# A decoder layer on one Trainium2 core: the stage behind the attention begun in its last units, and expert products with features along the partitions

## The chip, the core and the metric

The kernel runs on one core of a Trainium2 chip. Its engines are TensorE (PE, with its weight loads shown apart as PEld), VectorE (DVE), ScalarE (ACT), GpSimd (POOL) and SyncE (SP), which here only issues DMAs. The metric is the device time of one execution in microseconds. The kernel has a program of its own for each engine; the programs meet only at semaphores.

## What is computed

One decoder layer on x of 4 x 1024 tokens, 512 features, all in fp32, with three residual sums:

```
x = x + attention(layernorm(x))            # 16 heads of 64, rotary, causal; W_out 1024 -> 512
x = x + memory_read(layernorm(x), context) # a 32x32 matrix per head built from 64 context rows
                                           # by a recurrence; q normalised, read, Wo, bo
x = x + experts(layernorm(x))              # 8 experts, top 2 of them per token:
        ff_gate = ragged_dot(sorted_tokens, we_gate, group_sizes)
        ff_up = ragged_dot(sorted_tokens, we_up, group_sizes)
        activated = silu(ff_gate) * ff_up
        ff_out = ragged_dot(activated, we_down, group_sizes) * sorted_weights
        output = zeros.at[sorted_token_idx].add(ff_out)
```

Gate, up and down are 512 x 512 for each expert.

## The kernel before

Four stages stand in one launch: context, attention, memory, experts. Each ends with a meeting of all engines (L103 to L110). Tiles called early_... live across stages: early_xT, early_wq and early_wv (weights in split form), early_stage (raw weights), early_ident.

**Products.** An fp32 product is three fp32r products. ACT rounds an operand to a high half (Copy), DVE or POOL subtracts to get the low half, and PE adds high x high, high x low and low x high (three lines: L1601 to L1603 in the memory stage, L2068 to L2070 in the experts).

**Attention (a_...)** goes through U = 512 units: 64 head groups (hg) of 8 query tiles. A unit is scores (PE L950, L951), row maximum (DVE L1216), exponentials (ACT L1084), transposes (PE L962), copies (ACT L1095, DVE L1226) and values (PE L979, ACT L1101, DVE L1241). The queries and keys of a head group come from a_rot over 12 DMAs of 128 KB, which SP issues (`stack`, L677 and L681) up to a group ahead, into one of two buffers; scores of the group's first unit wait for all of them. POOL rotates queries and keys (L799, L806), runs the recurrence of the context rows (`context_row`, L850 to L864, ten instructions each, two rows in every 16 units, at units 11 and 14 of them), and at unit U-16 issues `load_next` (L840): the raw weights of the memory stage, six DMAs of 512 KB into early_stage. After the last unit POOL stores the memory matrix (L886). SP stores attention outputs to scr_attT and, per batch, the reciprocals of the row sums to scr_rinv (L696); ACT and DVE turn nothing of the next stage's data in this stage.

**Memory (m_...)** goes through 32 token tiles. For tile i: attention output and reciprocals come in (SP L1471, L1474, 1 MB together), POOL multiplies them (`att_scale`, L1550), ACT and DVE split the product into m_ap (L1706, L1798), PE multiplies by W_out (`att_out`, 24 matmuls of 128x512 in m_A), DVE adds x (L1844) and normalises (L1803 to L1812), PE transposes (`turn`, L1612), multiplies by Wq (m_Q), reads the memory, and so on to router and scatter. At the stage's head POOL writes constants (L1522 to L1544), ACT and DVE split four chunks of W_out in early_xT (L1700, L1776) and centre and split two chunks of Wq in early_wq and early_wv (L1784 to L1788, L1765, L1776). `att_out` of tile 0 waits for the split W_out and for m_ap.

**Experts (e_...)** go through NBLK = 39 blocks of 256 rows (two row tiles t). In a block, PE's order is gate(t0), up(t0), gate(t1), `turn_act`(t0), up(t1), `turn_rows`(t0), half of down(t0), `turn_act`(t1), rest of down(t0), `turn_rows`(t1), down(t1). Gate, up and down are 12 matmuls of 128x512 per row tile, 72 in a block; hT (rows, transposed) stands still and the weight moves. `turn_act` transposes the activation e_a (4 transposes) into PSUM, from where ACT and DVE split it into e_aT (L2136, L2187). `turn_rows` (L2076) transposes the next block's rows. ACT applies silu (L2146), splits the next weights (L2142) and scales the result (L2151); DVE multiplies (`mult`, L2199), splits weights (L2193), and makes the row numbers dest (L2233), which waits for the semaphore `added`, raised when the last block's rows have been added to the output. POOL fetches weights (L2030) and adds rows to the output (`add_rows`, L2034, from e_y and e_dest).

Of the kernel before, what the change touches and what calls it, by code (L numbers as in the profile page):

```python
# [47 lines left out]
def program(nc, io):  # L48
# [19 lines left out]
    with ExitStack() as keep:  # L68
# [5 lines left out]
            "ident": keep.enter_context(nc.sbuf_tensor("early_ident", [P, P], F32)),  # L74
        }
# [355 lines left out]
def attention_phase(nc, io, dram, scan, early):  # L431

    with Room(nc, "a_") as rm:
# [10 lines left out]
        rot = rm.sb("rot", [P, 4, T], F32R)  # L444
# [61 lines left out]
        s_wm = rm.sem("wm")  # L506
        s_scan = rm.sem("scan")
# [72 lines left out]
        def sums_turn(u):  # L580

            if u >= GU * G and u % (GU * G) == 4:
                return u // (GU * G) - 1
            return None


# [80 lines left out]
        def _(sp):  # L667
# [58 lines left out]
            for half in range(2):  # L726
                for b in range(B):
# [3 lines left out]
                                 ).then_inc(s_k2, 16)  # L731
            for u in range(U + 6):
                if values_turn(u - 1) is not None:
                    store(values_turn(u - 1))
                if u % (2 * QT) in (0, QT + 2) and 0 < u < U - QT:
                    stack(u // QT + 1)
                if sums_turn(u - 1) is not None:
                    store_sums(sums_turn(u - 1))
# [12 lines left out]
        def _(gp):  # L751
# [114 lines left out]
            for u in range(U):  # L866
# [12 lines left out]
                if u == U - 16:  # L879
                    load_next()  # L880
                if u == 9:
                    context_start()
                if u % (2 * QT) in (11, 14):
                    context_row(2 * (u // (2 * QT)) + u % (2 * QT) // 14)
            for a in range(2):
                gp.dma_start(dram["mem"][:, :, a * half:(a + 1) * half, :].rearrange("b h i j -> (b h) (i j)"),  # L886
                             M[a * 64:(a + 1) * 64, :, :].rearrange("p i j -> p (i j)")).then_inc(s_mem, 16)
            gp.wait_ge(s_mem, 32)
            gp.wait_ge(s_wm, 96)

# [153 lines left out]
        def _(act):  # L1044
# [61 lines left out]

            key_root(0)
# [6 lines left out]
            for u in range(U + 6):  # L1114
# [10 lines left out]
                for n, j in ends(v_steps(u - 1), 8):  # L1125
                    v_high(n, j)

        @block.vector
        def _(dve):
# [112 lines left out]

            key_variance()
# [10 lines left out]
            for u in range(U + 6):  # L1254
# [22 lines left out]
                if u < U:  # L1277
                    for p in splits(u):
                        if p[0] == "x":
                            x_low(p)  # L1280

# [7 lines left out]
def memory_phase(nc, io, dram, route, early):  # L1289
# [4 lines left out]
    with Room(nc, "m_") as rm:  # L1294
# [5 lines left out]
        ap = rm.sb("ap", [P, 2, 2, 8, P], F32R)  # L1300
# [32 lines left out]
        sd = rm.sb("sd", [P, 2])  # L1333
        rs = rm.sb("rs", [P, 2])
# [44 lines left out]
        def weights(a, k):  # L1379

            return early["xT"][:, a, k, :] if k < ET else (
                early["wq" if k == ET else "wv"][:, a, :, :].rearrange("p e n -> p (e n)"))
# [76 lines left out]
        def _(sp):  # L1459
# [35 lines left out]
            load_att(0, 0)  # L1495
            load_x(0, 0)
            for dst, src in ((bo[:, :], io["bo"].partition_broadcast(P)),
                             (wo[:, :, :], io["woT"].rearrange("(e p) n -> p e n", p=P))):
                sp.dma_start(dst, src).then_inc(s["c"], 16)
            load_att(0, 1)  # L1500
            load_x(0, 1)
# [794 lines left out]
```

## Time and profile before

| | us |
|---|---|
| median of three runs | 2873.59 |
| the runs | 2867.46, 2873.59, 2874.5 |
| the profiled execution | 2874.91 |
| its span | 2873.2 |
| PE busy, share of the span | 2665.0, 93% |
| DVE busy | 2000.5, 70% |
| ACT busy | 1620.8, 56% |
| POOL busy | 1468.0, 51% |

The span is the time between the first and the last recorded instruction; 1.7 us of the profiled execution lie around it. Time in rows is counted from the span's start. Attention ends and memory starts at about 1595; experts start at about 2131. A row of a timeline gives the start, the length, the engine, the line, the operation with its tiles, how many instructions of a kind follow in it, and in brackets how long the engine had been idle and for whom it waited. Matmuls are pipelined, so the next one starts before the end shown: what a matmul costs is the distance of two starts.

### The profile page before, as it was taken

Reading aid. Unit: us, or ns where it says so; the run is one execution under the profiler, and the core shown is the slowest. Engines: PE = TensorE matmul, PEld = TensorE weight load, DVE = VectorE, ACT = ScalarE, POOL = GpSimd, SP = SyncE. Lnnn points to the kernel's source line nnn. Section 1 sums busy time; section 2 is a strip of 40 time slices with the busy share of each in tenths; the row PEclk is TensorE's granted clock in tenths of the full one; section 3 lists DMA queues with packets and bytes.
Section 4 is the critical chain, followed back from the end, with each engine's and each line's share of the span. In section 5 each row is a group of like instructions: output and inputs, shape, how many; then the busy total and the mean of one; then the engine's idle time right before and its main releaser. Section 6 shows DMA issues by size and latency. Waiting matters only on the chain. (4 is left out here: it accounts for less than half of the span.)

```text
span 2873.2 us, 48962 instructions
## 1 busy us (share of the span) xinstructions
PE 2665.0 (93%) x15375; PEld 2267.7 (79%) x15375; DVE 2000.5 (70%) x4223; ACT 1620.8 (56%) x3157; POOL 1468.0 (51%) x1676
## 2 busy tenths in 40 slices
PE   7999989999899999899998599999959999999997
PEld 5888878888788888788887487877748888888886
DVE  6777766777667777677777688978846556666655
ACT  3666666666656666566666333333336666666665
POOL 3676646676647675556565333434323444343434
PEclk9999999999999999999999799999979999999999
DMA  6654544444544444444444654544334443444433
GB/s 175 106 122 106 123 103 98 118 113 104 132 96 99 115 107 114 103 109 100 94 91 114 170 135 134 158 134 147 96 126 96 102 87 74 102 99 100 100 52 51
DMA packets 192360, 316.56 MB, mean 110 GB/s; under 512 B 60496, under 2 KB 106224, under 8 KB 189104
## 3 DMA queue, kind: packets, MB, share of 16 engines
q1 hardware_dynamic: 148656, 216.86, 31.6%
q0 software_dynamic: 43520, 97.46, 13.9%
q8 instruction: 90, 1.47, 0.2%
q14 instruction: 94, 0.77, 0.1%
HBM read 241.08 MB, written 75.17 MB: 110 GB/s over the span
## 5 line engine op out<-in xcount | busy, mean ns | idle before, releaser
L1095 ACT ACTIVATE a_pt<-a_PT 128x512 fp32r<-128x512 f32 (+3 forms) x768 | 350.4, 491 | 449.9 <-PE a_PT L962 443.3
L1226 DVE TENSOR_TENSOR a_pt<-a_PT,a_pt 128x512 fp32r<-128x512 f32 (+3 forms) x768 | 401.5, 550 | 155.2 <-ACT a_pt L1095 150.7
L1216 DVE CUSTOM_DVE_ANT_0 a_S<-a_S,a_mask 128x1024 f32<-128x1024 f32 (+7 forms) x512 | 387.5, 757 | 72.5 <-PE a_S L951 71.1
L1084 ACT ACTIVATE a_pb<-a_S,a_nmax 128x1024 f32<-128x1024 f32 (+7 forms) x512 | 381.0, 744 | 36.5 <-DVE a_nmax L1216 36.5
L962 PE MATMUL a_PT<-early_ident,a_pb 128*128 128x128 f32 x2304 | 345.0, 276 | 51.2 <-DVE a_pt L1226 50.9
L962 PEld LDWEIGHTS a_PT<-early_ident,a_pb 128*128 128x128 f32 x2304 | 275.9, 142 | 112.4 <-issue 58.5
L979 PE MATMUL a_O<-a_pt,a_v 128*128 128x256 f32 (+1 forms) x2560 | 346.5, 283 | 17.8 <-DVE a_xt L1201 16.8
L979 PEld LDWEIGHTS a_O<-a_pt,a_v 128*128 128x128 f32 x2560 | 330.4, 193 | 31.2 <-DVE a_xt L1201 24.0
L2193 DVE TENSOR_TENSOR e_w<-early_stage,e_w 128x1024 fp32r<-128x1024 f32 x238 | 280.6, 1220 | 65.0 <-ACT e_w L2142 64.9
L950 PE MATMUL a_S<-a_kh,a_qs 128*128 128x512 f32 (+3 forms) x768 | 286.7, 373 | 10.6 <-DMA a_kl<-a_rot 8.8
L951 PE MATMUL a_S<-a_kl,a_qs 128*128 128x512 f32 (+3 forms) x768 | 259.0, 349 | 0.0
L2034 POOL DMA_INDIRECT out<-e_y,e_dest x78 | 158.3, 2029 | 183.5 <-ACT e_y L2151 157.5
L894 PE MATMUL a_Z<-early_xT,early_wq 128*128 128x512 f32 x512 | 226.1, 442 | 26.5 <-DVE early_stage L1189 18.4
L2142 ACT ACTIVATE e_w<-early_stage 128x2048 fp32r<-128x2048 f32 x120 | 229.2, 1911 | 31.5 <-DVEq L2177 19.3
L806 POOL TENSOR_TENSOR a_rot<-early_stage,a_rot 128x512 fp32r<-128x512 f32 x128 | 163.4, 1295 | 146.3 <-ACT a_rot L1066 146.1
L1241 DVE TENSOR_TENSOR a_ot<-a_O,a_otmp 64x256 f32<-64x256 f32 x256 | 106.2, 415 | 184.1 <-ACT a_otmp L1101 184.0
L2030 POOL DMA_INDIRECT early_stage<-in_we,e_ix x119 | 128.1, 1076 | 177.7 <-issue 163.5
L799 POOL TENSOR_TENSOR early_stage<-early_stage,a_part 128x512 f32<-128x512 f32 x64 | 82.6, 1291 | 265.8 <-DVE a_part L1189 265.7
L895 PE MATMUL a_Z<-early_xT,early_wq 128*128 128x512 f32 x512 | 203.2, 397 | 0.0
L896 PE MATMUL a_Z<-early_xT,early_wq 128*128 128x512 f32 x512 | 203.2, 397 | 0.0
L950 PEld LDWEIGHTS a_S<-a_kh,a_qs 128*128 128x128 f32 x768 | 147.4, 192 | 32.9 <-DMA a_kl<-a_rot 12.3
L951 PEld LDWEIGHTS a_S<-a_kl,a_qs 128*128 128x128 f32 x768 | 147.5, 192 | 17.1
(305 smaller groups left out, 6890.2 us busy)
## 6 DMA issues: line engine op xcount, KB each, us to landing
a_qs<-a_rot SPq DMA_DIRECT2D x256, 128.0 KB, 2.4
a_kh<-a_rot SPq DMA_DIRECT2D x256, 128.0 KB, 2.4
a_kl<-a_rot SPq DMA_DIRECT2D x256, 128.0 KB, 2.4
e_rows<-scr_hs SPq DMA_DIRECT2D x40, 516.0 KB
scr_attT<-a_ot SPq DMA_DIRECT2D x256, 64.0 KB, 2.2
m_att<-scr_attT SPq DMA_DIRECT2D x32, 512.0 KB
m_rb<-scr_rinv SPq DMA_DIRECT2D x64, 256.0 KB
early_stage<-in_wqk POOLq DMA_DIRECT2D x31, 512.0 KB
```

The costliest lines, as they stand in the source:

```text
L894: pe.matmul(out, lhs(0), rhs(0), start=start, stop=False)
L895: pe.matmul(out, lhs(0), rhs(1), start=False, stop=False)
L950: pe.matmul(out, q, kh[:, sl, c0:c1], start=True, stop=False)
L951: mm = pe.matmul(out, q, kl[:, sl, c0:c1], start=False, stop=True)
L962: mm = pe.transpose(PT[(k + s) % 2][:, (kt % 4) * P:(kt % 4 + 1) * P], pb[u % 2][:, kt * P:(kt + 1) * P], ident[:, :])
L979: mm = pe.matmul(O[:, c0:2 * P], v2[:, n % 2, kt, h, :, :].rearrange("p a d -> p (a d)"), pt[j % 2][:, part, kt, c0:2 * P], start=kt == 0 ...
L1084: act.activation(pb[u % 2][:, 0:cols], S[u % 2][:, 0:cols], ACT.Exp, bias=nmax[:, u % GU:u % GU + 1], scale=-1.0, accum_out=rsum[:, b % 2, ...
L1095: act.activation(pt[u % 2][:, 0, 4 * s:4 * s + m, (qt % 2) * P:(qt % 2 + 1) * P], PT[(k + s) % 2][:, 0:m * P].rearrange("p (k q) -> p k q" ...
L1216: dve.tensor_tensor_reduce(out=sc, in0=sc, in1=mask[:, T - cols:T], scale=-1.0, scalar=-MASKED, op0=ALU.add, op1=ALU.min, accum_out=nmax[: ...
L1226: dve.tensor_tensor(pt[u % 2][:, 1, 4 * s:4 * s + m, q], PT[(k + s) % 2][:, 0:m * P].rearrange("p (k q) -> p k q", k=m), pt[u % 2][:, 0, 4 ...
L2142: act.activation(w[:, k, 0, :], raw[:, k, :], ACT.Copy).then_inc(s[f"whi{k}"], 1)
L2193: dve.tensor_tensor(w[:, k, 1, c], raw[:, k, c], w[:, k, 0, c].bitcast(F32), ALU.subtract).then_inc(s[f"wlo{k}"], 1)
```

## The change

Three groups of edits; line numbers in orders "after" are those of the changed kernel.

**1. The attention's last units.** a_rot becomes early_rot and is kept; in the memory stage it is `ap`. SP loads attention outputs and reciprocals of tiles 0 and 1 at units U-13 and U-11, POOL multiplies them at U-8 and U-6, ACT and DVE split them into early_rot behind the last units. Four chunks of W_out are split at U-7 to U+1, the high half by ACT, the low half by POOL. Four context rows move into earlier 16-unit stretches (24 to 27), so that the last one stands at U-34 and the store of the matrix at U-32. The reciprocals of the last batch are turned and stored two units earlier.

```diff
+        ROWS_AT = [u for u in range(U) if u % (2 * QT) in (11, 14) or
+                   u % (2 * QT) == 2 and 24 <= u // (2 * QT) < 28][:TC]
+        FRONT_IN = (U - 13, U - 11)
+        FRONT_SCALE = (U - 8, U - 6)
+        TAIL_HIGH = (U - 7, U - 5, U - 3, U - 1)
+        TAIL_LOW = (U - 5, U - 3, U - 1, U + 1)
...
+            def tail_low(k):
+                gp.wait_ge(s_wmhi, k + 1)
+                gp.tensor_tensor(xT[:, 1, k, :], tail(k), xT[:, 0, k, :].bitcast(F32),
+                                 ALU.subtract).then_inc(s_wmlo, 1)
...
+            def tail_high(k):
+                act.wait_ge(s_wm, 96)
+                act.activation(xT[:, 0, k, :], tail(k), ACT.Copy).then_inc(s_wmhi, 1)
+
+            def front_high(j):
+                act.wait_ge(s_fscale, j + 1)
+                for sl in range(2):
+                    act.wait_ge(s_stack[sl], 192 * (NG * GH // 2))
+                act.activation(front[:, j, 0, :, :], front_rows(j), ACT.Copy).then_inc(s_fhi, 1)
```

On POOL, near the attention's end, the rows L864 and L852 to L862 are context rows, early_stage<-in_wmem is `load_next`, L806 (now L860) the low half of the last rotation. Before:

```order
1106 L864 TENSOR_TENSOR scan_keys<-scan_keys 128x512
1107 L840 DMA early_stage<-in_wmem 128x1024 x6
1108 L852 TENSOR_TENSOR scan_keys<-scan_keys,scan_k 128x512
...
1127 L864 TENSOR_TENSOR scan_keys<-scan_keys 128x512
1128 L886 DMA scr_mem<-scan_keys 64x512 x2
```

After:

```order
1120 L918 TENSOR_TENSOR scan_keys<-scan_keys 128x512
1121 L956 DMA scr_mem<-scan_keys 64x512 x2
...
1126 L854 TENSOR_TENSOR early_stage<-early_stage,a_part 128x512
1127 L860 TENSOR_TENSOR early_rot<-early_stage,early_rot 128x512 x2
1128 L894 DMA early_stage<-in_wmem 128x1024 x6
1129 L923 TENSOR_TENSOR a_xt<-a_xt,early_wq 128x1024
1130 L923 TENSOR_TENSOR a_part<-a_part,early_wq 128x1024
1131 L928 TENSOR_TENSOR early_xT<-early_stage,early_xT 128x1024 x4
```

No context row stands between the last rotation and `load_next` any more; two multiplications and four subtractions stand behind it.

**2. The head of the memory stage.** PE no longer waits there for the split W_out nor for POOL's constants; tiles 0 and 1 are neither loaded, multiplied nor split; only the two chunks of Wq are centred and split. The raw weights of the first expert are fetched at tile 2. ACT applies one root first, which loads its table. On PE, behind `att_out` of tile 0 (24 matmuls), the transposes of tile 0's normalised rows stood ahead of `att_out` of tile 1. Before:

```order
6243 L1603 MATMUL m_A<-early_xT,m_ap 128x512
6244 L1612 MATMUL m_T<-early_ident,m_n 128x128 x4
6245 L1601 MATMUL m_A<-early_xT,m_ap 128x512
```

After:

```order
6243 L1693 MATMUL m_A<-early_xT,early_rot 128x512
6244 L1691 MATMUL m_A<-early_xT,early_rot 128x512
...
6255 L1693 MATMUL m_A<-early_xT,early_rot 128x512
6256 L1702 MATMUL m_T<-early_ident,m_n 128x128 x4
6257 L1691 MATMUL m_A<-early_xT,early_rot 128x512
```

They stand behind 12 of the second tile's 24 matmuls now.

**3. The experts.** Gate and up are computed with their features along the partitions: a 128x128 piece of the weight stands still, the 256 transposed rows move. `turn_act` goes; the activation is split from SBUF, in halves h of the features. Down is cut into four pieces of six matmuls.

```diff
-                for e in range(ET):
-                    mm = parts(out[t][:, :], lambda a: hT[:, t, a, e * P:(e + 1) * P],
-                               lambda a: w[:, k, a, e * D:(e + 1) * D], e)
+                for f in range(2 * h, 2 * h + 2):
+                    for e in range(ET):
+                        c = e * D + f * P
+                        mm = parts(out[h][:, f % 2 * BLK:(f % 2 + 1) * BLK], lambda a: w[:, k, a, c:c + P],
+                                   lambda a: hT[:, a, e, :], e)
...
                 product(j, 0, pG, 0, "G")
+                product(j, 0, pG, 1, "G")
                 product(j, 1, pU, 0, "U")
-                product(j, 0, pG, 1, "G")
-                turn_act(j, 0)
                 product(j, 1, pU, 1, "U")
+                down(j, 0, 0)
                 turn_rows(j + 1, 0)
-                down(j, 0, 0, 2)
-                turn_act(j, 1)
-                down(j, 0, 2, ET).then_inc(s["Y"], 1)
+                down(j, 1, 0)
                 turn_rows(j + 1, 1)
-                down(j, 1, 0, ET).then_inc(s["Y"], 1)
+                down(j, 0, 1)
+                down(j, 1, 1)
...
+            def act_high(j, h):
+                act.wait_ge(s["mul"], 2 * j + h + 1 + CR)
+                act.wait_ge(s["Y"], 2 * j + CR)
+                act.activation(aT[:, 0, 2 * h:2 * h + 2, :], a32[:, h, :].rearrange("p (f r) -> p f r", f=2),
+                               ACT.Copy).then_inc(s["ahi"], 1)
...
+            def act_low(j, h):
+                dve.wait_ge(s["ahi"], 2 * j + h + 1)
+                f = slice(2 * h, 2 * h + 2)
+                dve.tensor_tensor(aT[:, 1, f, :], a32[:, h, :].rearrange("p (f r) -> p f r", f=2),
+                                  aT[:, 0, f, :].bitcast(F32), ALU.subtract).then_inc(s["alo"], 1)
```

On PE, the end of the up product in the last block (before: up(t1) comes after `turn_act`(t0), L2083). Before:

```order
7157 L2070 MATMUL e_G<-e_w,e_hT 128x512
7158 L2083 MATMUL e_T<-early_ident,e_a 128x128 x4
7159 L2068 MATMUL e_U<-e_w,e_hT 128x512
```

After:

```order
7215 L2158 MATMUL e_U<-e_hT,e_w 128x256
7216 L2159 MATMUL e_U<-e_hT,e_w 128x256
7217 L2184 REGISTER_ALU
7218 L2157 MATMUL e_Y<-e_w,e_aT 128x512
```

The matmuls of gate and up are half as wide and twice as many, 96 in a block, and down follows them with no transposes of e_a between. On DVE, one block's loop, first the multiplication. Before:

```order
3042 L2199 TENSOR_TENSOR e_a<-e_U,e_sil 128x512
3043 L2187 TENSOR_TENSOR e_aT<-e_T,e_aT 128x512
...
3046 L2199 TENSOR_TENSOR e_a<-e_U,e_sil 128x512
3047 L2233 CAST e_dest<-e_nxt 128x2
```

After:

```order
3042 L2287 TENSOR_TENSOR e_a<-e_U,e_sil 128x512
3043 L2275 TENSOR_TENSOR e_aT<-e_a,e_aT 128x512
3044 L2320 CAST e_dest<-e_nxt 128x2
...
3051 L2281 TENSOR_TENSOR e_w<-early_stage,e_w 128x1024
3052 L2285 REGISTER_ALU
3053 L2287 TENSOR_TENSOR e_a<-e_U,e_sil 128x512
3054 L2275 TENSOR_TENSOR e_aT<-e_a,e_aT 128x512
```

dest, with its wait for `added`, and half a weight split stand ahead of the second multiplication now. On POOL the fetch of the gate weight stands ahead of the first `add_rows`.

## Rows read from the trace of the kernel before

**Rows 1.** The page: busy us, share of the span, instructions by engine.
```profile
PE 2665.0 (93%) x15375; PEld 2267.7 (79%) x15375; DVE 2000.5 (70%) x4223; ACT 1620.8 (56%) x3157; POOL 1468.0 (51%) x1676
```

**Rows 2.** Timeline of PE, one expert block: start us, length us, engine, line, operation.
```profile
2400.12 0.39 PE L2068 MATMUL e_G<-e_w,e_hT 128*128 128x512 f32 x1
...
2402.91 0.60 PE L2083 MATMUL e_T<-early_ident,e_a 128*128 128x128 f32 x4
2403.27 0.48 PE L2068 MATMUL e_U<-e_w,e_hT 128*128 128x512 f32 x1
2403.58 0.40 PE L2069 MATMUL e_U<-e_w,e_hT 128*128 128x512 f32 x1
...
2418.64 0.39 PE L2068 MATMUL e_G<-e_w,e_hT 128*128 128x512 f32 x1
```

**Rows 3.** Timeline of PE, 256-column matmuls with a new stationary operand each.
```profile
59.97 0.28 PE L896 MATMUL a_Z<-early_wv,early_xT 128*128 128x256 f32 x1
...
62.49 0.28 PE L896 MATMUL a_Z<-early_wv,early_xT 128*128 128x256 f32 x1
```

**Rows 4.** Timeline of DVE in the same expert block.
```profile
2406.44 0.69 DVE L2199 TENSOR_TENSOR e_a<-e_U,e_sil 128x512 f32<-128x512 f32 x1 [1.52 <-PE e_U L2070]
2407.05 0.16 DVE L2233 CAST e_dest<-e_nxt 128x2 int32<-128x2 f32 x1
...
2407.67 1.22 DVE L2193 TENSOR_TENSOR e_w<-early_stage,e_w 128x1024 fp32r<-128x1024 f32 x1
```

**Rows 5.** The line L2034, add_rows: from issue to landing, us.
```profile
DMA to landing us min/median/max: 4.6/4.9/9.5
```

**Rows 6.** Timeline of the memory stage's head, POOL, PE and DVE.
```profile
1595.23 0.52 POOL L1522 MEMSET m_bd<- 128x512 f32 x1 [29.97 <-POOLq L110]
...
1607.58 0.76 PE L1601 MATMUL m_A<-early_xT,m_ap 128*128 128x512 f32 x1 [16.91 <-DVE m_ap L1798]
...
1615.06 0.40 PE L1603 MATMUL m_A<-early_xT,m_ap 128*128 128x512 f32 x1
1623.55 1.11 PE L1612 MATMUL m_T<-early_ident,m_n 128*128 128x128 f32 x4 [8.09 <-DVE m_n L1812]
...
1632.37 0.69 DVE L1844 TENSOR_TENSOR m_x<-m_A,m_x 128x512 f32<-128x512 f32 x1 [4.87 <-PE m_A L1603]
...
1634.68 2.35 DVE L1812 TENSOR_SCALAR m_n<-m_x,m_mv,m_rs 128x512 f32<-128x512 f32 x1
```

**Rows 7.** Windows: length; PE, PEld, DVE, ACT, POOL busy; PEclk; DMA share; GB/s.
```profile
1607.00:1611.00 4.00, 3.42 (x8) 2.77 (x9) 3.90 (x5) 0.88 (x1) 0.00 (x0) 0.50 1.13 192
```

**Rows 8.** Timeline near the attention's end, POOL, SP (DMA issues) and PE.
```profile
1533.20 1.26 POOL L852 TENSOR_TENSOR scan_keys<-scan_keys,scan_k 128x512 f32<-128x512 f32 x1
...
1547.04 3.20 POOL L840 DMA_DIRECT2D early_stage<-in_wmem  x6 [0.30 <-POOL scan_keys L864]
...
1533.27 0.57 SPq L677 DMA_DIRECT2D a_qs<-a_rot  x1
...
1539.59 1.22 SPq L681 DMA_DIRECT2D a_kl<-a_rot  x2
...
1542.65 0.50 PE L950 MATMUL a_S<-a_kh,a_qs 128*128 128x512 f32 x1
```

**Rows 9.** From issue to landing: a_kl issued 1549 to 1554, then the six wmem DMAs.
```profile
DMA to landing us min/median/max: 7.9/8.6/9.7
...
DMA to landing us min/median/max: 5.0/10.6/15.5
```

**Rows 10.** Timeline of PE and DVE, first units of the last two head groups.
```profile
1562.91 0.50 PE L950 MATMUL a_S<-a_kh,a_qs 128*128 128x512 f32 x1 [2.82 <-DMA a_kl<-a_rot]
...
1543.88 1.23 DVE L1216 CUSTOM_DVE_ANT_0 a_S<-a_S,a_mask 128x1024 f32<-128x1024 f32 x1
...
1549.02 1.10 DVE L1216 CUSTOM_DVE_ANT_0 a_S<-a_S,a_mask 128x896 f32<-128x896 f32 x1
...
1564.15 1.23 DVE L1216 CUSTOM_DVE_ANT_0 a_S<-a_S,a_mask 128x1024 f32<-128x1024 f32 x1 [2.88 <-PE a_S L951]
...
1571.36 1.10 DVE L1216 CUSTOM_DVE_ANT_0 a_S<-a_S,a_mask 128x896 f32<-128x896 f32 x1 [0.71 <-PE a_S L951]
```

**Rows 11.** Timeline of ACT: a split of 128x1024, then an attention copy.
```profile
1605.17 1.06 ACT L1706 ACTIVATE m_ap<-m_att 128x1024 fp32r<-128x1024 f32 x1 [5.83 <-issue]
...
1579.23 0.38 ACT L1101 ACTIVATE a_otmp<-a_O 64x256 f32<-64x256 f32 x1 [0.72 <-PE a_O L979]
```

More of the change, by code:

```diff
@@ L74, in program @@
             "ident": keep.enter_context(nc.sbuf_tensor("early_ident", [P, P], F32)),
+            "rot": keep.enter_context(nc.sbuf_tensor("early_rot", [P, 4, T], F32R)),
         }
@@ L506, in attention_phase @@
         s_wm = rm.sem("wm")
+        s_wmhi = rm.sem("wmhi")
+        s_wmlo = rm.sem("wmlo")
+        s_first = [rm.sem(f"first{i}") for i in range(2)]
+        s_fscale = rm.sem("fscale")
+        s_fhi = rm.sem("fhi")
+        s_flo = rm.sem("flo")
         s_scan = rm.sem("scan")
@@ L580, in sums_turn, with front_rows, front_sums, tail @@
         def sums_turn(u):
-            if u >= GU * G and u % (GU * G) == 4:
+            if u == U + 2:
+                return B - 1
+            if GU * G <= u < U and u % (GU * G) == 4:
                 return u // (GU * G) - 1
             return None
+        front = rot[:, :, :].rearrange("p (j a) (f t) -> p j a f t", j=2, t=P)
+        def front_rows(j):
+            return (xt[:, :, :, :].rearrange("p a e t -> p (a e) t") if j == 0 else
+                    part[:, :, :].rearrange("p a (f t) -> p (a f) t", t=P))
+        def front_sums(j):
+            return wq[:, j, :, :].rearrange("p e n -> p (e n)").bitcast(F32)
+        def tail(k):
+            return stage[:, k // 2, k % 2 * T:(k % 2 + 1) * T]
+        ROWS_AT = [u for u in range(U) if u % (2 * QT) in (11, 14) or
[4 more added lines that the diff above has]
+        TAIL_LOW = (U - 5, U - 3, U - 1, U + 1)
         def values_done(u):
@@ L1562, in step @@
                     gp.tensor_tensor(x2b[:, i % 4, :], x2[:, i % 2, :], bo[:, :], ALU.add).then_inc(s["x2b"], 1)
-                if here(r, i + 2):
+                if here(r, i + 2) and after(r, i + 2, 3):
                     att_scale(r, i + 2)
+                if isinstance(r, int) and t == 2:
+                    gp.wait_ge(s["wl"], 2)
+                    for k in range(3):
+                        gp.dma_start(route["raw"][:, k, :], io["we"][0, k]).then_inc(s["pre"], 16)
                 if here(r, i - 4):
@@ L1633, in memory @@
                               ).then_inc(s["mwp"], 1)
-                if here(r, i - 1):
+                second = isinstance(r, int) and r * QT + i == 1
+                if here(r, i - 1) and not second:
                     turn("n", 1, n2[:, (i - 1) % 2, :], "n2")
@@ L1697, in _ @@
             act.sem_inc(s["hT"], CR)
-            act.sem_inc(s["ahi"], CR)
-            for k in range(4):
-                act.activation(weights(0, k), loaded(k), ACT.Copy).then_inc(s["wh"], 1)
-            act.wait_ge(s["pool"], 18)
+            act.sem_inc(s["ahi"], CR + 2)
+            act.activation(root[:, :], ident[:, 0:1], ACT.Sqrt)
             def att_high(r, j):
                 t = r * QT + j
-                act.wait_ge(s["an"], t + 1)
+                act.wait_ge(s["an"], t - 1)
                 act.wait_ge(s["x2"], t - 1 + CR)
@@ L1736, in step @@
                 memory_high(1)
-                if here(r, i + 1):
+                if here(r, i + 1) and after(r, i + 1, 2):
                     att_high(r, i + 1)
@@ L1836, in step @@
                 memory_low(1)
-                if here(r, i + 1):
+                if here(r, i + 1) and after(r, i + 1, 2):
                     att_low(r, i + 1)
@@ L2048, in _ @@
                 point(j + 2)
-                wait_alone(gp, s["y"], 2 * j + 1 + CR, s["any"])
-                add_rows(0)
                 wait_alone(gp, s["ix"], j + 2, s["any"])
@@ L2053, in _ @@
                 fetch(0)
+                wait_alone(gp, s["y"], 2 * j + 1 + CR, s["any"])
+                add_rows(0)
                 wait_alone(gp, s["y"], 2 * j + 2 + CR, s["any"])
```

193 lines of the change are left out of this document (108 added, 85 removed).

## The prediction, made before the changed kernel ran

> **What bounds the kernel now.** I read the page first: PE is busy for 2665.0 of 2873.2 us, 93%, and the next engine, DVE, for 70% [rows 1]. So time is to be had in two ways only: from waits of PE, or from the work that PE does. Then the timeline of PE in the three places that the change touches. In the experts the matmuls follow each other without a gap [rows 2]: that stage is bound by PE's own work, and only fewer or cheaper matmuls shorten it. At the head of the memory stage PE stands still for 16.91 and then 8.09 us [rows 6]: there the chain POOL, ACT, DVE is the bound. Near the attention's end PE waits once, 2.82 us, for the keys of the last head group [rows 10], and the transfers are what counts there. The rest of the program is not changed in anything that PE waits for.
>
> **The experts.** A block lasts from 2400.12 to 2418.64, 18.52 us [rows 2]. From the first gate matmul to the transposes there are 12 matmuls in 2.79 us, 0.233 each. From the start of the four transposes to the second matmul behind them it is 0.67, of which 0.233 is the first matmul's: a group of transposes costs 0.44. With 72 matmuls and four groups, 72 x 0.233 + 4 x 0.44 = 18.54, the block as measured.
> The change makes 48 of the 72 into 96 of 256 columns, each with a weight piece of its own to load. The context of such matmuls is in the trace: 21 of them in a row from 59.97 to 62.49, 0.120 apart [rows 3], their loads hidden. So 96 x 0.120 = 11.52 in place of 48 x 0.233 = 11.18: the turned products cost 0.34 more. The two groups of `turn_act` go, 0.88. The new block is 11.52 + 24 x 0.233 + 2 x 0.44 = 17.99, 0.54 less; 39 blocks give **-21.0**. If each narrow matmul took just half a wide one, 0.1165, it would be another 0.34 less per block, 13 in all; if 0.123, 0.29 more, 11 in all. I take 0.120, which is the same form and the same shape.
> This holds if the split of the activation is in time, because the transposes and halves that covered it are gone. From the block's start: G ends at 5.76, U's first half at 8.64, its second at 11.52. `mult` starts 0.3 behind the half's end and lasts 0.69 [rows 4], to 9.6; the high half on ACT takes about 0.6 (1.06 for twice the size [rows 11]), the low half on DVE 0.7, done at about 11.0. down starts at 11.52: 0.5 spare. DVE then makes dest (0.62 from there to the weight split, 1.22 for that) [rows 4], to 12.7; the second `mult` ends at 13.4, high 14.1, low 14.8. The down pieces that need it start behind two pieces of six (1.40 each) and two groups of transposes: 11.52 + 2.80 + 0.88 = 15.2. Spare, 0.35. This is the thinnest cover of the change: what DVE does later than so is lost in each block. The last rows of the next block are split at about 17.2, wanted at 18.0.
> The `added` signal moves ahead of the second `mult` on DVE; behind it in DVE's queue wait the weight split, `mult`, and through them ACT's splits and down. I place the issue of the second `add_rows` at 4.5 us into the next block (two row results on ACT behind the block's end, then two adds on POOL), an estimate, and its landing 4.9 later (4.6 to 9.5) [rows 5], 9.4. DVE reaches the wait at about 10.9. 1.5 spare, 1.8 until PE waits.
>
> **The head of the memory stage.** Nothing that `att_out` of tile 0 needs is made in the stage any more, so PE starts within 0.3 us of the stage's first record at 1595.23, not at 1607.58 [rows 6]. It starts at half clock as before: 8 matmuls in the window 1607 to 1611 stood 0.43 apart with PEclk 0.50 [rows 7], which is 1.2 of 2.4 GHz, after PE had been idle. The 24 matmuls then take 7.7 as before (1607.58 to 1615.3) and end at 1603.3. Half of tile 1 follows at once, 12 x 0.233 = 2.8, to 1606.1. Meanwhile DVE adds x and normalises: for tile 1 it was 2.3 from the addition at 1632.37 to the last step at 1634.68, and 2.35 for that step [rows 6]. From 1603.9 on this gives 1606.6 (a last step of 0.4) to 1608.6. Transposes 0.4, 12 more matmuls 2.8: tile 1 is out at about 1610.5, where before it was at 1632.37 [rows 6]. I take 21.9 less 0.6 for the normalising step: **-21.3**. The bounds: 17, if DVE's steps are all held up beside POOL and PE falls back to half clock for a piece (12 x 0.2 = 2.4 and 2); 24, if the clock rises earlier. Waits that stand later in the stage are as before, and both chains begin from tile 1.
> The rule against it: 2.35 us for a normalising step of 128x512 on DVE [rows 6], while POOL multiplied, where the addition of 128x512 took 0.69. By the Trainium skill, page SBUF — State Buffer, section Who interferes with whom, DVE and GpSimd share a pair of SBUF ports, and the one that comes second fully blocks until the first has finished. The rows agree. By it the changed stage, where POOL multiplies tile 2 at about 1604 to 1607, loses the same 2 us again.
>
> **The attention's end.** Here the change moves work into a stretch in which PE has little idle time.
> (a) `load_next` moves. Before, it stood behind two context rows on POOL and issued at 1547.04; these rows started at 1533.20, when the last rotation was done [rows 8]. Now nothing stands between, and the six DMAs (3 MB) issue at 1533.3, together with SP's 12 DMAs of head group 62 (1533.27 to 1540.8), whose keys PE wanted at 1542.65 and had [rows 8]. What the two do to each other is seen one head group later: the last four of group 63's key DMAs, issued beside wmem, landed 7.9 to 9.7 us after their issue, the first at 1557.4, the last at 1562.9, with a query DMA among them: five steps of 1.1 us; wmem's took 5.0 to 15.5 [rows 9], from 1552.0 to 1565.2, 2.6 us for each 512 KB. At 1.1 us group 62's 12 are complete at 1546.5, at 1.25 (the first ones wait for the queue to fill) at 1548.3, which I take. PE waits 5.6 us at 1542.65. Behind the wait of before PE ran at half clock and two units took 7.21 us (1564.15 to 1571.36) where they had taken 5.14 (1543.88 to 1549.02) [rows 10]: 2.1 more. Together +7.7.
> (b) In return the old wait goes: wmem has landed at about 1551, well ahead of group 63: -2.8 - 2.1 = -4.9 [rows 10].
> (c) Four high halves on ACT, 1.06 each [rows 11], stand ahead of attention copies that PE waits for. Idle time of ACT hides the first; ACT had 0.7 idle ahead of the copy at 1579.23 [rows 11] and less at its neighbours, so I count 0.7, 0.3 and 1.0 for the others: +2.0. Nothing at the lower end, 4 x 1.06 = 4.2 at the upper.
> (d) Everything else lies beside waits: POOL's six steps (2.4 each, idle there), the front loads (2 MB, when no keys are in flight), the splits into early_rot behind the last units. The stage's end hangs on the stores of the last outputs, as before: 0.
> Sum **+4.8**, from -4.9 (no wait at all, ACT hidden) to +9.
>
> **The rivals.**
> (A) Group 62 is hardly late. SP's keys issue one by one, and if the two streams share the engines equally, keys have their full share: 512 KB in 2.6 us and 128 KB in 1.1 [rows 9] are 200 and 119 GB/s, half of the sum is 160, and the group's 1.57 MB at that take 9.9 us, so they are there at 1543.2 to 1545. Wait 1 to 2.5 us plus clock: +3 or so in place of 7.7, time 2874.9 - 1.3 + 0.1 - 42.3 = 2831. Against it: group 63 saw 1.1 us per DMA, which is 12 x 1.1 = 13.2. Chance 0.22. The Trainium skill, DMA: Bandwidth & Descriptors, section Queues, rings and completion order, states that each engine goes round robin between queue rows packet by packet, which speaks for such an equal share; the time by it would be this rival's.
> (B) The split of the activation is late for the second half of down. Decides from 0.35 us over my chain, for instance by a slower `mult` or by ACT still in its weight split (1.9 us) when `mult` ends. At 0.5 us lost in each block, +20: 2856. Chance 0.12.
> (C) Slower than before: `added` comes late in every block. It decides from 1.8 us later than placed, at 11.2 in the block. Each further us costs 39. From 2.8 us late (over 12.2) the experts lose what all has gained; were every add as long as the longest, 9.5 [rows 5], it would be the landing 4.6 later and 2.8 x 39 = 109 more, 2945. For it: the longest landing is that long, and POOL's queue has a new order. Against: the median is 4.9. Chance 0.03.
> (D) The head gives only 17: 2840, inside the range. Chance 0.13.
> (E) The 256-column matmuls don't keep their rate over 96 in a row, 0.123 or more: +11, 2847. Chance 0.10.
>
> **How the numbers follow.** 2874.9 + 4.8 - 21.3 - 21.0 = 2837.4 for the profiled execution, which lies 1.3 above the median of the runs: **2836**, chance of the sum as it stands 0.40, the rivals have the rest. The range 2823 to 2852 holds the sum with all bounds of the attention's end and the head (2836 - 13 for A with a quicker head and narrow matmuls at half a wide one's; 2836 + 16 for D or E with an attention's end of +9), and leaves out B in its full size, and C: 0.8. About 0.3% or 8.6 us is what a measurement can tell from no change. Faster (below 2865) 0.92; within 0.3% 0.05, from B with more than 0.7 us per block; slower 0.03, C.
>
> **What would show it.** After: expert blocks 18.0 us apart, gate and up matmuls 0.12 apart, no wait of PE for DVE's e_aT at the third piece of down, and none of DVE at dest. Memory: PE's first matmul within 1 us of the barrier, tile 1 added at about T + 15, T being the stage's start. Attention: PE idle for a_kl at the first unit of group 62, not of 63; group 62's DMAs landing over 7 us after their issue. Wrong it would be if PE waits in each block, or if the stage's start T itself moves by more than 6.

## The result, and the profile after

| | before | after |
|---|---|---|
| median, us | 2874.05 (4 runs) | 2835.12 (4 runs) |
| lowest to highest | 2867.46 to 2880.41 | 2831.72 to 2842.36 |
| profiled execution | 2874.91 | 2831.72 |
| its span | 2873.2 | 2830.0 |

The ratio is 0.9874, 95% interval 0.9856 to 0.9893: 1.3% faster. The forecast was 2836. The two profiled executions are 43.2 us apart, 4 more than the medians. I cut both spans at four places that exist in both: the row maximum of unit U-17, the memory stage's first record (T), the addition of x to tile 1 in that stage, and the first transposes of the experts.

| stretch | before | after | difference | forecast |
|---|---|---|---|---|
| start to unit U-17 | 1542.30 | 1537.65 | -4.65 | 0 |
| U-17 to T | 52.93 | 59.78 | +6.85 | +4.8 |
| T to tile 1 | 37.14 | 16.92 | -20.22 | -21.3 |
| tile 1 to the experts | 496.00 | 496.94 | +0.94 | 0 |
| the experts | 744.83 | 718.71 | -26.12 | -21.0 |

Ahead of unit U-17 only the places of four context rows differ; what the first line is worth is taken up below.

**The attention's end.** Timelines of POOL, SP and PE of the changed kernel, and the landing of the last two key DMAs of group 62; they answer to [rows 8, 9].

```profile
1529.17 3.19 POOL L894 DMA_DIRECT2D early_stage<-in_wmem  x6 [0.57 <-issue]
...
1528.63 0.57 SPq L709 DMA_DIRECT2D a_qs<-early_rot  x1
...
1535.41 1.23 SPq L713 DMA_DIRECT2D a_kl<-early_rot  x2
...
1547.25 0.79 PE L1021 MATMUL a_S<-a_kh,a_qs 128*128 128x512 f32 x1 [9.19 <-DMA a_kl<-early_rot]
```

```profile
DMA to landing us min/median/max: 10.8/11.0/11.2
```

The six weight DMAs and group 62's twelve start together, as the order said. The keys' last DMA, out at about 1536, lands 11.2 later, and PE waits 9.19 us, for which 5.6 had been forecast. The DMAs of both queues in the stretch 1534 to 1546, with packets and bytes of each queue (q0 carries POOL's weights, q1 SP's keys):

```profile
DMA packets 1037, 3.34 MB, mean 278 GB/s; under 512 B 217, under 2 KB 225, under 8 KB 1036
q0 software_dynamic: 556, 2.02, 61.8%
q1 hardware_dynamic: 480, 1.31, 41.0%
```

The weights got 2.02 of 3.34 MB, the keys 1.31: 61% and 39%.

One group later, where before had its wait [rows 10], there is none; timeline of DVE:

```profile
1549.37 1.23 DVE L1301 CUSTOM_DVE_ANT_0 a_S<-a_S,a_mask 128x1024 f32<-128x1024 f32 x1 [10.13 <-PE a_S L1022]
...
1565.58 0.69 DVE L1301 CUSTOM_DVE_ANT_0 a_S<-a_S,a_mask 128x512 f32<-128x512 f32 x1
1567.09 1.22 DVE L1301 CUSTOM_DVE_ANT_0 a_S<-a_S,a_mask 128x1024 f32<-128x1024 f32 x1
...
1572.46 1.08 DVE L1301 CUSTOM_DVE_ANT_0 a_S<-a_S,a_mask 128x896 f32<-128x896 f32 x1
```

From U-16 (1549.37) to U-8 (1567.09) it is 17.72 us, against 20.27 in before.

**The head of the memory stage.** POOL, PE and DVE, to be held beside [rows 6].

```profile
1597.43 0.52 POOL L1612 MEMSET m_bd<- 128x512 f32 x1 [9.11 <-POOLq L111]
...
1598.18 0.80 PE L1691 MATMUL m_A<-early_xT,early_rot 128*128 128x512 f32 x1 [5.17 <-DVEq L1863]
...
1607.39 2.36 POOL L1640 TENSOR_TENSOR m_att<-m_att,m_rb 128x1024 f32<-128x1024 f32 x1 [4.63 <-DMA m_rb<-scr_rinv]
...
1608.73 1.30 DVE L1900 TENSOR_SCALAR m_n<-m_x,m_mv,m_rs 128x512 f32<-128x512 f32 x1
...
1610.09 0.66 PE L1702 MATMUL m_T<-early_ident,m_n 128*128 128x128 f32 x4 [1.82 <-DVE m_n L1900]
...
1614.35 0.68 DVE L1932 TENSOR_TENSOR m_x<-m_A,m_x 128x512 f32<-128x512 f32 x1
...
1616.64 2.33 DVE L1900 TENSOR_SCALAR m_n<-m_x,m_mv,m_rs 128x512 f32<-128x512 f32 x1
```

PE begins 0.75 behind T in place of 12.35. The normalising step of tile 0 ends at 1610.03, 0.3 behind POOL's multiplication (1607.39 + 2.36), and PE waits 1.82 for it. Tile 1's normalising step takes 2.33, again beside POOL's multiplication; it lies behind the cut at tile 1.

**The experts.** PE in one block, which answers to [rows 2]:

```profile
2384.82 0.28 PE L2157 MATMUL e_G<-e_hT,e_w 128*128 128x256 f32 x1
2384.94 0.28 PE L2158 MATMUL e_G<-e_hT,e_w 128*128 128x256 f32 x1
2385.06 0.28 PE L2159 MATMUL e_G<-e_hT,e_w 128*128 128x256 f32 x1
...
2399.42 0.60 PE L2165 MATMUL e_T<-early_ident,e_rows 128*128 128x128 f32 x4
2399.77 0.48 PE L2157 MATMUL e_Y<-e_w,e_aT 128*128 128x512 f32 x1
...
2402.65 0.28 PE L2157 MATMUL e_G<-e_hT,e_w 128*128 128x256 f32 x1
```

A block takes 17.83 us (2384.82 to 2402.65) where it took 18.52. The 96 narrow matmuls fill 2384.82 to 2396.18, 0.1183 each and not 0.120. The same block on DVE, beside [rows 4]:

```profile
2395.71 0.16 DVE L2320 CAST e_dest<-e_nxt 128x2 int32<-128x2 f32 x1
...
2398.85 0.69 DVE L2275 TENSOR_TENSOR e_aT<-e_a,e_aT 128x512 fp32r<-128x512 f32 x1 [0.70 <-ACT e_aT L2221]
```

dest waits for nothing in this block. In one of the 39 it does, the block from 2581.0, and the wait reaches PE; DVE and PE:

```profile
2593.36 0.17 DVE L2320 CAST e_dest<-e_nxt 128x2 int32<-128x2 f32 x1 [1.43 <-POOLq L2149]
...
2597.30 0.50 PE L2157 MATMUL e_Y<-e_w,e_aT 128*128 128x512 f32 x1 [1.15 <-DVE e_aT L2275]
```

That block takes 19.25 us. In the block shown first, the second low half ends at 2399.54, and the piece of down that reads it starts at 2399.77: 0.23 spare, 0.35 had been forecast.

### The profile page after: what moved, and what is told of

It is laid out like the page before. It is cut to its first block and busy times, and to the rows that moved or that the text cites. A ratio compares the mean times of both kernels' runs of the same rounds, so it can differ in the third digit from the quotient of the medians.

```text
span 2830.0 us, 51945 instructions
## 1 busy us (share of the span) xinstructions
PE 2634.6 (93%) x16935; PEld 2329.1 (82%) x16935; DVE 1996.4 (71%) x4219; ACT 1617.9 (57%) x3158; POOL 1498.4 (53%) x1680
## 5 line engine op out<-in xcount | busy, mean ns | idle before, releaser
L860 POOL TENSOR_TENSOR early_rot<-early_stage,early_rot 128x512 fp32r<-128x512 f32 x128 | 163.4, 1295 | 125.2 <-ACT early_rot L1137 124.8
L2123 POOL DMA_INDIRECT out<-e_y,e_dest x78 | 181.8, 2330 | 36.7 <-ACT e_y L2237 18.7
L2157 PE MATMUL e_G<-e_hT,e_w 128*128 128x256 f32 x624 | 177.2, 284 | 1.5 <-DVE e_hT L2269 1.5
L2158 PE MATMUL e_G<-e_hT,e_w 128*128 128x256 f32 x624 | 176.7, 283 | 0.0
```

What stands on the lines that cost most here:

```text
L2157: pe.matmul(out, lhs(0), rhs(0), start=k == 0, stop=False)
L2158: pe.matmul(out, lhs(0), rhs(1), start=False, stop=False)
```

## The experiments

Medians are of four or five executions (ten for e6). Each ratio is against the kernel before, run beside it on the same chip, with its 95% interval; so two kernels measured on different chips are compared by their ratios. Where a kernel's own profile says more than its time, the stretches of the table above are used, since they leave out the attention's first 1540 us.

**One group of edits at a time.** e1 is the kernel before with the expert function of the changed one; e2 is the changed kernel with the expert function of before.

> The kernel before with the third group of edits alone (the experts). If the groups are independent and the experts' gain is PE's own work, blocks of 17.83 us in place of 18.53 stand here too: -0.70 x 39 = -27, about 2847 against 2874 of before, and nothing moves ahead of the experts. Rival: part of the 26 us that the experts' stage gained in the profile of the changed kernel comes from the earlier groups (weights fetched at another time, another start); then it is less than 24 here.

> The changed kernel with the experts of before: groups 1 and 2 alone. The profile gives +6.8 for the attention's end and -20.2 for the head of the memory stage, so 13.4 less than before, about 2860.5. Rival: the 4.6 us by which the attention ran ahead in the changed kernel's profile, in code that is the same, belong to the change as well; then 18 less, 2856, and the shift is seen again before unit U-17.

e1: 2851.47 us against 2872.55, ratio 0.9926 (0.9912 to 0.9939), 21 less. e2: 2862.76 against the same, ratio 0.9966 (0.9952 to 0.9979), 10 less. The two add to 31 where the whole change gave 39; each of these differences is uncertain by 4. By its time e1 gained less than the 24 at which my rival would hold. The stage decides against the rival: the experts are 717.75 us in e1 (718.71 after, 744.83 before, and 744.5 in e2, which has the old experts), so the 26 us are the experts' own. Why e1's median shows 21 and not 27 isn't settled; the profiled execution of e1, 2846.48, is among the fastest of its five. In e2 U-17 to T is 61.59 and T to tile 1 is 16.09, again like the changed kernel.

These profiles also bear on the 4.65 us. Unit U-17 has its row maximum at 1542.30 in before, 1544.57 in e1, 1542.97 in e2 and 1537.65 after; in e3 to e9 it is at 1538.2 to 1545.7. The context rows have their old places in before and e1, the new ones in all the others. The nine with the new places lie on both sides of the two with the old ones and 8 us apart, so 4.65 is inside the scatter of executions; that a microsecond or two of it is the change's can't be excluded. My rival for e2 also wanted 18 us less, and it was 10. The fast start of this one profile accounts for its 43 us where the medians show 39.

**What the wait for group 62 is.** e3 issues the six weight DMAs from SP, behind the group's keys, and no longer from POOL beside them; e4 leaves them on POOL, but behind a wait for the keys' landing.

```diff
                     stack(u // QT + 1)
+                    if u // QT + 1 == NG * GH - 2:
+                        load_next()          # e3: the same six DMAs, issued by SP
```
```diff
                 gp.wait_ge(s_wlow, len(wcount))
+                gp.wait_ge(s_stack[0], 192 * (NG * GH // 2))   # e4
```

> The changed kernel, but load_next's six DMAs are issued by SP directly behind the 12 DMAs of group 62, on the same queue, in place of POOL beside them. If the wait of 9.2 us at U-16 and 1.3 us behind it are all contention, they go: group 62 lands by 1538 as in before, wmem by about 1547, group 63 by about 1553, wanted at 1555. PE waits for no keys: 10.5 less than the changed kernel, about 2824.5. Rival: the six DMAs stand ahead of group 63 and of output stores on SP, so the wait comes back at U-8 with some 5 us, 2829.5, or the stores hold up PE.

> The changed kernel, but load_next on POOL waits until group 62's keys have landed. It then issues at about 1538.5, beside group 63 (from 1539.4). If two queues slow each other whichever group it is, group 63 lands 18 us after its first issue, at about 1557, wanted at 1555.4: a short wait at U-8, as in before, with its half clock: -10.5 + 2 to 4.9, about 2827 to 2829.5. Rival, that the keys have an equal share of the engines: group 63 in time, no wait, 2824.5.

e3: 2826.29 us against 2872.55, ratio 0.9838 (0.9825 to 0.9852), about 9 less than the changed kernel. U-17 to T is 48.72 us, 11.1 less than after. PE's waits from 1540 to 1600 in e3 name no keys:

```profile
PE a_PT L1033 <- DVE a_pt L1311: 9.6, 10, 2.0
PE m_A L1691 <- DVEq L1863: 5.4, 1, 5.4
PE a_O L1050 <- DVE a_ot L1326: 0.7, 1, 0.7
PE a_S L1021 <- ACT a_pb L1155: 0.6, 2, 0.4
```

So the wait at U-16 was the two streams side by side. The keys land after 2.3 to 2.8 us, and the six weight DMAs behind them on the same queue land 1.2 to 1.5 us apart, where on a queue of their own beside the keys it had been 2.3 to 3.4. The same stretch in e1, with the attention of before, is 49.04 us, with a key wait of 0.9 in it. The new work on ACT, POOL and DVE is to be read behind all key waits, from U-6 to T: 23.9 and 24.2 us in before and e1, 24.4 to 25.9 (25.0 in the middle) in the nine profiles that have that work. It costs about 1 us, where I had counted 2.0.

e4: 2828.65 us, ratio 0.9841 (0.9821 to 0.9861), from 2817.42 to 2837.22, the widest scatter of all. Its profile is of the slowest of the five, and in it the wait is back at U-8:

```profile
1546.16 3.18 POOL L895 DMA_DIRECT2D early_stage<-in_wmem  x6 [10.16 <-DMA a_kl<-early_rot]
...
1566.54 0.53 PE L1022 MATMUL a_S<-a_kh,a_qs 128*128 128x512 f32 x1 [3.20 <-DMA a_kl<-early_rot]
```

The last four key DMAs of group 63 (a_kl) landed 10.1 to 11.8 us after their issue. This is the mechanism of before, and the rival of e4 falls in this execution. How much of it arrives varies: in e1, with the attention of before word for word, the weights again went out 3.0 us behind group 63's first DMA (1546.31 and 1549.32; 1544.04 and 1547.04 in before), but SP had the twelve out in 8.1 us and not in 9.7, and PE waited 0.86 us and not 2.82; that the one caused the other isn't shown. U-17 to T was 49.04 in e1 and 52.93 in before. So the -4.9 of my sum stood in one profile of before and is 1 or less in another; the changed kernel's 9.2 at U-16, on the other hand, is 9.37, 9.18 and 9.25 in e2, e5 and e6.

**The clock behind the wait.** The four profiles with the wait at U-16 agree in the wait and differ in what comes behind it. PE's granted clock fell to 0.50 in the wait in all of them. In after it was back at about 1550.5, 3.2 us after PE had begun again, and the two units U-16 to U-14 took 5.55 us (5.56 in e5). In e2 it was back only at about 1561.7, 8.9 us after PE had begun again, and the two units took 7.44 (7.70 in e6). DVE and a window in e2; the clock is the third number from the end:

```profile
1554.87 1.23 DVE L1301 CUSTOM_DVE_ANT_0 a_S<-a_S,a_mask 128x1024 f32<-128x1024 f32 x1 [10.30 <-PE a_S L1022]
...
1562.31 1.10 DVE L1301 CUSTOM_DVE_ANT_0 a_S<-a_S,a_mask 128x896 f32<-128x896 f32 x1 [0.38 <-PE a_S L1022]
...
1552.70:1561.00 8.30, 6.93 (x28) 6.28 (x29) 3.14 (x7) 2.81 (x7) 0.00 (x0) 0.50 0.86 206
```

U-17 to T is 61.59 and 61.47 in e2 and e6, 59.78 and 59.95 in after and e5. Why the clock came back early in two executions and late in two isn't shown.

**How thin the cover in the experts is.** e5 puts one more multiplication of 128x512 (into a spare tile) on DVE ahead of the second `mult` of each block; e6 puts a memset of 128x2560 on POOL ahead of the first `add_rows`.

```diff
                 weight_low(j + 1, 0, 0)
+                dve.wait_ge(s["spr"], j + 1)
+                dve.tensor_tensor(spare[:, :], pU[0][:, :], sil[:, 0, :], ALU.mult).then_inc(s["spr"], 1)
                 mult(j, 1)
```
```diff
                 wait_alone(gp, s["y"], 2 * j + 1 + CR, s["any"])
+                wait_alone(gp, s["spr"], j + 1, s["any"])
+                gp.memset(spare[:, :], 0.0).then_inc(s["spr"], 1)
                 add_rows(0)
```

> The changed kernel with one more multiplication of 128x512 on DVE (into a spare tile) ahead of the second mult of each block, 0.69 us with its own wait. In the profile of the changed kernel the low half of the second e_aT ends at 2399.54 and the piece of down that reads it starts at 2399.77: 0.23 spare. If DVE's chain is as thin as that, each block gets 0.7 - 0.25 = 0.4 to 0.5 us longer, 18.25 to 18.3 in place of 17.83, and PE waits for e_aT in each: +16 to +19, about 2853. Rival: the spare time is larger than it looks (PE's queue is ahead of the records), block unchanged, 2835.

> The changed kernel with a memset of 128x2560 (about 2.4 us) on POOL ahead of the first add_rows of each block, which moves both adds and the signal added 2.4 us back. In the profile the second add issues at 2406.64 and lands 5.7 later (median), 2412.3, and DVE reaches the wait at 2413.55: 1.2 spare on DVE and 0.2 on PE behind it. If added is the next limit, DVE waits at dest in each block for 1.2 us and a block gets about 1.0 longer: 18.8, +38, about 2873. Rival: POOL has time of its own there and the adds overlap, so that less than 1 us of the 2.4 arrives: under +10.

e5: 2850.47 us against 2870.34, ratio 0.9939 (0.9916 to 0.9961). The median block is 18.29 us, 0.46 longer, for 0.61 us more on DVE (the `mult` starts 0.61 after the extra one): 0.15 was spare. PE waits for e_aT in 38 of 39 blocks. In the profile each wait is small (9.2 us in all over the stage) though the blocks grew by 18: ahead of the piece of down stand the four transposes, whose row is 0.60 long while the next matmul can start 0.35 behind their start, so the first 0.25 us of each wait doesn't show as idle time. A wait of this kind is better read from the distance of blocks.

```profile
PE e_Y L2158 <- DVE e_aT L2277: 9.2, 38, 1.1
```

e6: 2870.31 us against 2870.34, ratio 0.9990 (0.9978 to 1.0002): 2.27 us of POOL's time per block give back the whole gain of the change. DVE now waits where it did not:

```profile
DVE e_dest L2324 <- POOLq L2153: 32.4, 28, 3.1
```
```profile
PE e_Y L2161 <- DVE e_aT L2279: 23.8, 26, 2.8
```

The blocks take 18.71 on average, from 17.83 to 22.4. This is rival C of the forecast, brought about on purpose: of 2.27 us on POOL 0.88 reach the average block, so `added` has 1 to 1.4 us to spare. With one size of delay the slope beyond that isn't measured.

**DVE beside POOL.** e7 is e3 with POOL waiting, for tiles 0 and 1 of the memory stage, until DVE has normalised the tile.

```diff
                     gp.wait_ge(s["x2"], t + 1 + CR)
+                    if isinstance(r, int) and t == 1:
+                        gp.wait_ge(s["n2"], 2)
...
+            gp.wait_ge(s["n2"], 1)
             att_scale(0, 2)
```

> The kernel of e3_load_behind_keys with POOL waiting, for tiles 0 and 1 of the memory stage, until DVE has normalised the tile, before it multiplies or adds. If the normalising step of 2.36 and 2.35 us is one of 0.55 held up by POOL's instruction, it takes 0.55 here, PE's waits for m_n (2.91 and 1.96) shrink by 1.8 each, and the time is some 3 less than e3, about 2823, unless POOL's later multiplication of tile 2 is missed: that is the rival, PE waits for m_ap of tile 2 instead and nothing is won.

e7: 2820.26 us against 2870.34, ratio 0.9825 (0.9810 to 0.9839); e3 had 0.9838 (0.9825 to 0.9852), which the times don't tell apart from it. The step, in e3 and then in e7, tile 0 and tile 1, with POOL's multiplications beside them:

```profile
1604.05 2.34 POOL L1640 TENSOR_TENSOR m_att<-m_att,m_rb 128x1024 f32<-128x1024 f32 x1 [5.71 <-DMA m_rb<-scr_rinv]
...
1604.31 2.36 DVE L1900 TENSOR_SCALAR m_n<-m_x,m_mv,m_rs 128x512 f32<-128x512 f32 x1
...
1613.78 2.36 POOL L1640 TENSOR_TENSOR m_att<-m_att,m_rb 128x1024 f32<-128x1024 f32 x1
...
1614.07 2.35 DVE L1900 TENSOR_SCALAR m_n<-m_x,m_mv,m_rs 128x512 f32<-128x512 f32 x1
```
```profile
1604.58 0.55 DVE L1903 TENSOR_SCALAR m_n<-m_x,m_mv,m_rs 128x512 f32<-128x512 f32 x1
...
1605.21 2.39 POOL L1640 TENSOR_TENSOR m_att<-m_att,m_rb 128x1024 f32<-128x1024 f32 x1 [6.60 <-DVE m_n L1903]
...
1612.17 0.55 DVE L1903 TENSOR_SCALAR m_n<-m_x,m_mv,m_rs 128x512 f32<-128x512 f32 x1
```

0.55 us alone, 2.36 with POOL's multiplication begun 0.26 earlier, and the end lies 0.28 behind POOL's end. So it does in all nine steps of tiles 0 and 1 that POOL held in after, e3, e4, e5 and e6 (0.28 or 0.29), whatever their length, 1.15 to 2.36. The Trainium skill, page SBUF — State Buffer, section Who interferes with whom, gives the rule: DVE instructions in the modes that use both ports, which `tensor_scalar` can enter, share a pair of ports with GpSimd, and the one that issues second fully blocks. These rows agree with it to 0.3 us.

What the order buys is another matter. From T to tile 1 it is 16.59 in e7 and 18.75 in e3, but 16.1 to 17.2 in after, e2, e4, e5 and e6, which don't have the wait: e3's profile had met the worst case in tile 0. PE's waits for m_n went from 2.91 and 1.96 to 0.58 and 1.38, not by 1.8 each. The step of tile 1 tells more. Where POOL held it (after, e3, e4, e6: 2.33 to 2.35), T to the experts takes 513.9 to 516.5 us. Where it took 0.55 by the new order (e7, e8, e9), it takes 511.3, 513.6 and 509.0; where it took 0.55 by chance (e2, e5), 510.2 and 509.8. In e2 POOL's multiplication came just behind the step:

```profile
1622.95 0.55 DVE L1900 TENSOR_SCALAR m_n<-m_x,m_mv,m_rs 128x512 f32<-128x512 f32 x1
...
1623.55 2.38 POOL L1640 TENSOR_TENSOR m_att<-m_att,m_rb 128x1024 f32<-128x1024 f32 x1 [0.86 <-DMA m_rb<-scr_rinv]
```

So the order makes sure of some 3 to 4 us that an execution otherwise has or has not. That is read from nine profiles; the medians don't show it.

e7's own profile shows a price of the burst. Output stores that SP issued behind the six DMAs landed 10.7 to 11.8 us after their issue, and DVE waited for one:

```profile
1539.94 2.25 SPq L732 DMA_DIRECT2D scr_attT<-a_ot  x3
...
1551.83 0.42 DVE L1326 TENSOR_TENSOR a_ot<-a_O,a_otmp 64x256 f32<-64x256 f32 x1 [3.97 <-DMA scr_attT<-a_ot]
```

Stores are as late beside the weights on the other queue (11.2 to 12.7 us in after, 10.5 and 10.9 in before), but no DVE wait for one stands in those profiles. And e3, with e7's order of DMAs, had its first three stores in 7.4 to 8.1 and no such wait, so it differs between executions.

e8 therefore issues three of the six behind group 62 and three behind group 63; e9 is e7 once more, beside it.

> The kernel of e7_pool_after_norm with the six weight DMAs in two threes on SP's queue, one behind group 62's keys and one behind group 63's. In e7's profile two output stores behind all six landed 11.4 and 11.8 us after their issue and DVE waited 4.0 for one, PE 3.4 behind it. With half the load ahead the stores should land within 8 us, no wait of DVE for scr_attT, and the time is up to 4 less than e7 in executions that had the wait: 2817 to 2820. Rival: the second three delay the front loads of 2 MB behind them, POOL's multiplications and the splits come later, and the stage's end moves by 1 to 3 us.

> The kernel of e7_pool_after_norm again, beside e8 on the same chip, so that the two can be compared: 2820 by what it had. If the wait for an output store is a matter of the execution, this profile may be without it.

e8: 2824.11 us, 2822.6 to 2827.25, ratio 0.9832 (0.9817 to 0.9847). e9: 2823.86 us, 2819.58 to 2830.35, ratio 0.9837 (0.9820 to 0.9853), both against 2873.42. e9 is slower than e7 by its ratio and within its interval. The stores land after 4.6 to 9.8 us in e8, and DVE waits for none (1.4 us in e9, 4.0 in e7), but the times can't be told apart. U-17 to T is 49.20 in e8, 50.14 in e9, 55.08 in e7. The rival of e8, that the front loads come later and move the stage's end, isn't seen: U-6 to T is 24.9 in e8 and 25.0 in e9. e8 removes the long wait in its profile; that it is faster isn't shown. Either beats the changed kernel (0.9874) by 0.4%, that is by some 11 us.

## Why the forecast was right

- **The experts, -21.0, was -26.1.** The mechanism held: no waits of PE, two groups of transposes gone, narrow matmuls with hidden loads. The term of the sum that was off is the narrow matmul: 0.1183 us and not the 0.120 of [rows 3]. 96 x 0.0017 x 39 = 6.4, which is more than all of the 5.1. I had named this end (0.1165, another -13) and taken the row of the same shape. Why 256 columns cost 0.120 in one place and 0.1183 in the other isn't settled; both have a weight load each, and no run was made on it.
- **The head, -21.3, was -20.2.** PE's start came 0.75 behind T, not 0.3; the step of DVE behind POOL's multiplication was at 1.30, inside the 0.4 to 2.35 that I had given it. In the executions recorded it is anything from 0.55 to 2.36, by when POOL begins, so that this term came out near is in part luck. The rule against the change, the loss of 2 us beside POOL, held in full for tile 1 (2.33), whose step lies behind this stretch, as it did in before (2.35).
- **The attention's end, +4.8, was +6.85.** Three terms were mis-sized and in part cancel. Term (a), +7.7, was +10.55: between the two profiles the row maximum falls back by 10.14 at U-16 and by 0.41 more at U-15.
  The wait was 9.19, not 5.6. The step that failed is "12 x 1.25". The first three DMAs of the group landed 2.4, 4.8 and 8.3 us after the group's first issue; only the nine behind them came 1.0 to 1.4 us apart, and the last landed at 18.6. The same stretch in the trace of before, 1544.04 to 1562.9, was 18.8 us and would have given the answer directly. I also misread a row: the first of the four landings behind "five steps of 1.1 us" was at 1558.0 and not at 1557.4, so with the query DMA among them they are four steps of 1.2.
  The clock behind the wait cost 0.4 in this profile and not 2.1, but 2.3 and 2.6 in e2 and e6: that term was well sized for two executions of four.
  Term (b), -4.9, was -4.8 in this pair of profiles. Term (c), +2.0, was 1.1 between the two profiles (from U-6 to T) and about 1 over all of them. Against e1 in place of before, which lacks the long wait at U-8, the changed kernel's end costs 10.7 and not 6.85, and e2's 12.6: how large this term is depends on the executions compared.
- **The sign of being wrong.** I had said that the forecast would be wrong if T itself moved by more than 6. T moved by 2.2, but only because this execution was 4.65 ahead at U-17; in the stretch that the change touches it moved by 6.85, in e2 by 8.7. By what the sign was meant to catch, it was met: the attention's end was forecast too cheap.
- **Rival A** (an equal share for the keys, a wait of 1 to 2.5) fell: 9.19, and 10.1 to 11.8 us to land in e4. From 1534 to 1546 the weights' queue moved 168 GB/s and the keys' 109, together 278 in place of the 320 that the rival had added up. The page of the Trainium skill that spoke for it (DMA: Bandwidth & Descriptors, Queues, rings and completion order) states turns by packet; equal shares of the bytes did not come of it here.
- **Rival B** (the split late for down) was near: 0.15 to 0.23 us of cover, 0.35 forecast; e5 puts the price at 0.46 us per block for 0.61 us of DVE. **Rival C** (`added` late in every block) did not come: 1.2 us to spare, where 1.5 had been forecast. But it came in one block of 39, for 1.4 us (in one or two in e1, e4 and e8), which the sign "none of DVE at dest" had excluded. **Rival D** (the head gives only 17) fell with 20.2. **Rival E** fell to the other side.
- That the forecast time was met to 1 us is luck. For the profiled execution I had 2837.4, and it took 2831.7: the experts gave 5.1 us more, the attention's end cost 2.0 more, the head gave 1.1 less and the tiles behind it took 0.9 more, and the scatter ahead of U-17 took 4.65 off; the medians then lie 4 us nearer to each other than the profiles. The single terms were good to 1 to 5 us in this pair of profiles.

## What to carry to other kernels

Before a burst of transfers is moved, look for the last place where the same two streams ran side by side, and take the whole distance from first issue to last landing there, not a rate; then ask whether one queue, in the order in which the data are wanted, would do without the meeting at all (here 9 us of 2835, by e3). Turning a product so that its result lies as the next one wants it pays if the narrower matmuls keep their rate, but it takes the cover from the engine that prepares the operand: measure the spare time that is left (0.2 us here) before anything is added there. A step that always ends by the same distance behind another engine's instruction, at up to four times its own length, is held by it; whether an order between the two pays is read from several profiles, since single ones meet the collision or miss it.

## What the runs showed of the hardware

- Matmuls in a row, each with a stationary piece of its own to load: 0.1183 us per 128x256 in the experts, 0.120 in the context stage, 0.233 per 128x512. Half the width cost 0.51 of the time.
- A DVE step of 128x512 with scalar operands takes 0.55 us alone and 2.36 beside a POOL multiplication of 128x1024 that had begun 0.26 earlier. In nine of nine held steps it ends 0.28 or 0.29 behind POOL's instruction.
- 3 MB of weights (512 KB each) and 1.5 MB of keys (128 KB each) on two queues: keys from the fourth on 7.6 to 11.2 us from issue to landing, against 2.3 to 2.8 alone; 278 GB/s in all, 61% of it the weights'. Weights behind the keys on one queue: keys as alone, 371 GB/s from 1544 to 1552 in e3, output stores of 64 KB behind the weights 7.4 to 11.8 us. What part of the lower sum is the mix and what part the keys' own isn't shown.
- In a wait of 9.2 to 9.4 us the granted clock fell to 0.50, and it was back 3.2 us after PE had begun again in one execution and 8.9 in another; two units of attention took 5.6 and 7.4 to 7.7 us, with 5.1 where no wait stood ahead.
- In the same code, 1540 us long, nine profiled executions differ by up to 8 us (1537.65 to 1545.7): a difference of 5 us between two profiles says nothing until it is found in a stretch.
